# Layer two of a mixture-of-experts kernel: first tile's first two column blocks reordered, last tile computed and stored in halves on three queues

## The chip, the cores and the metric

The kernel runs on one core of one Trainium2 chip. The metric is device microseconds of one execution, median of several; lower is better. The profiled execution is a further one, with the hardware profiler on.

## What is computed

4096 tokens of width 256 pass two layers. Layer one mixes channels, routes each token to two of four experts (capacity 1024 each, exact GELU), and adds the result to x. Layer two, the one that is changed, is a gated feed-forward network whose three matrices each have a low-rank addition that is chosen per sample (32 tokens have one adapter):

```
def _lora_linear(x, W, A, B, adapter_indices):
    base = jnp.einsum('bsd,df->bsf', x, W)
    lora = jnp.einsum('bsr,brf->bsf', jnp.einsum('bsd,bdr->bsr', x, A[adapter_indices]), B[adapter_indices])
    return base + lora
gate = _lora_linear(x, Wg, Ag, Bg, adapter_indices)      # 256 -> 1024, rank 16
up = _lora_linear(x, Wu, Au, Bu, adapter_indices)
h = jax.nn.silu(gate) * up
cond = _lora_linear(h, Wd, Ad, Bd, adapter_indices)      # 1024 -> 256
x = x + (cond @ (weight * scale_weight[:, None]).T + bias)
```

## The kernel before, in words

Every engine has its instruction list written out by hand in its own function; semaphores tie them together. Nothing is scheduled by a tool: the order in the code is the order on the engine.

Layer two takes the tokens in 8 tiles of 512 (BT), sorted by adapter so that a tile has at most two adapters. A tile's 1024 hidden columns are taken in 8 column blocks of 128 (KH). The last linear layer is folded into Wd beforehand. Every float32 product is made of three matmuls, high part by high part, high by low, low by high (`product`, L1207 to L1213), so a block's gate costs 6 matmuls of 512 columns (two halves k of the 256 inputs), its up 6, each plus one low-rank matmul (`pair_half`, L1458), and its part of the down product another 6 (`down1_`).

PSUM has 8 banks of 128x512. Gate blocks alternate between banks 0 and 1, up blocks between 2 and 3, the tile's output (two halves of 128 rows) is gathered in banks 4 and 5, bank 6 takes the low-rank part of down, bank 7 the transposes and the low-rank product `um` of the next tile.

**Start of layer two.** The first tile's input x1T[0] is layer one's last output. PE forms it by 16 matmuls with a 0/1 matrix `pick` (`from_last`, L1517) into banks 0 and 1, DVE adds the token rows (L1190), ACT makes the high part x1s_hi (L717), DVE the low part x1s_lo (L1121). Then PE works through block 0 (banks 0 and 2: L1528, L1529, L1535), the low-rank product (`low_rank`, L1432, L1433, into bank 7), block 1's gate (bank 1) and up (bank 3), with block 0's and 1's `pair_half` in between. The moving operands of `pair_half`, ug and uu, are made from bank 7: DVE masks it (um, L1116), ACT copies 32-row pieces of um into four row groups (three copies for ug, L695 to L697, then three for uu), DVE subtracts to get one further row group of each (L1133). The gate of a block goes through Silu on ACT (L705), DVE multiplies it with the up block (prod, L1168), and splits it in two (L1172, L1174). Block 2 reuses bank 0, so PE waits for the first product before it.

**End of layer two.** After the last tile's blocks PE makes the low-rank down product (`low_rank_down`, L1423), the down product of blocks 6 and 7, and the closing low-rank matmuls (`finish`, L1480 to L1482). DVE adds the bias and x1T (`finish_out`, L1151) into out_sb, one instruction for each half of the rows. Then `last_stores` stores 16 samples (32 tokens each, 256 rows of 32 floats, 32 KB) with one DMA each to a place read from a table: 8 from SP's queue, 8 from ACT's, all behind the same wait on out_ev. POOL is done by then; its DMAs, all indirect gathers and scatters (L458, L469, L488, L496, L504, L518), end some 75 us before the end. SP ends the program when all stores have landed.

The names printed by the profile leave buffer numbers out, and its x_sb, x_rows, x_first in this layer are the code's x1_sb, x1_rows, x1_first.

## Time and profile before

| | us |
|---|---|
| median of 3 runs | 615.31 |
| lowest and highest run | 614.7, 615.56 |
| the profiled execution's own time | 613.93 |
| its span, first to last instruction | 612.1 |
| PE busy in the span | 580.1 (95%) |
| DVE, ACT, POOL busy | 355.0, 241.9, 146.3 |
| mean granted TensorE clock | 0.974 |

The profiled execution is 1.83 us longer than its span, and 1.38 us below the median of the runs. Busy time is summed over instructions; matmuls overlap their neighbours, so that a row's duration of 0.39 us is longer than the distance to the next matmul, and it is the distance that counts. PEld is the load of the stationary operand.

### The profile page before, as it was taken

The numbers are of one execution on the slowest core, as the hardware profiler recorded it, in microseconds if no ns is written. First come the engines' busy times: TensorE is split into PE (matmuls) and PEld (weight loads), VectorE is DVE, ScalarE is ACT, GpSimd is POOL, SyncE is SP. The second block draws the span as 40 slices with busy tenths as digits, with TensorE's granted clock in tenths as the row PEclk, the third lists the DMA queues.
The fourth block names the chain that finished last, engine by engine and source line by source line (L and its number), as shares of the span: only waits on it lengthen the run. The fifth ranks groups of instructions, "written<-read, shape, count | busy, mean of one in ns | idle before, by whom it ended". The sixth has DMA issues, their size and how long they took to land.

```text
span 612.1 us, 9927 instructions
## 1 busy us (share of the span) xinstructions
PE 580.1 (95%) x3438; PEld 476.8 (78%) x3438; DVE 355.0 (58%) x794; ACT 241.9 (40%) x532; POOL 146.3 (24%) x127
## 2 busy tenths in 40 slices
PE   5777699999999999999999999999999999999995
PEld 3645589999999999987878878878788788788783
DVE  6888655875677566655545545544465454544533
ACT  2643146755874764654412412313224133123010
POOL 3000222463454451757004003031040040100000
PEclk9976889999999999999999999999999999999998
DMA  9995749335329321653004105023041050130012
GB/s 326 343 288 180 289 147 325 46 107 136 36 74 315 44 49 22 128 115 95 9 1 138 18 0 146 12 90 66 0 135 19 0 142 13 43 74 6 12 24 34
DMA packets 64988, 61.95 MB, mean 101 GB/s; under 512 B 37616, under 2 KB 56816, under 8 KB 63600
## 3 DMA queue, kind: packets, MB, share of 16 engines
q1 hardware_dynamic: 53168, 37.99, 20.7%
q0 software_dynamic: 9600, 23.14, 15.7%
q10 hardware_dynamic: 2176, 0.26, 0.3%
q8 instruction: 24, 0.39, 0.3%
q14 instruction: 20, 0.16, 0.1%
HBM read 46.10 MB, written 19.47 MB: 107 GB/s over the span
## 4 chain that ended last, share of the span: by engine, by line
PE 87%; DVE 6%; DMA 3%; ACT 1%; issue 1%; SPq 1%; DVEq 0%; POOLq 0%
PE bank L1211 25%; PE bank L1212 24%; PE bank L1213 24%; PE bank L1458 5%; PE bank L1423 2%; DMA xT<-in_xT 2%; DVE passed L862 1%; DMA xg<-flat_rows,slot_row 1%; PE bank L1283 1%; PE bank L1415 1%; PE bank L1319 1%; PE bank L1310 1%; PE bank L1432 1%; PE bank L1433 1%; PE bank L1517 1%
## 5 line engine op out<-in xcount | busy, mean ns | idle before, releaser
L705 ACT ACTIVATE act<-bank 128x512 f32<-128x512 f32 x64 | 38.3, 598 | 189.2 <-PE bank L1458 189.2
L1168 DVE TENSOR_TENSOR prod<-bank,act 128x512 f32<-128x512 f32 x64 | 44.2, 690 | 99.4 <-PE bank L1458 97.3
L1071 DVE TENSOR_TENSOR hid_lo<-hf,hid_hi 128x512 fp32r<-128x512 f32 (+1 forms) x72 | 45.5, 633 | 53.6 <-ACT hf L641 53.3
L1211 PE MATMUL bank<-w_hi,hid_hi 128*128 128x256 f32 x256 | 71.8, 280 | 0.0
L1212 PE MATMUL bank<-w_lo,hid_hi 128*128 128x256 f32 x256 | 71.4, 279 | 0.0
L1213 PE MATMUL bank<-w_hi,hid_lo 128*128 128x256 f32 x256 | 71.3, 279 | 0.0
L638 ACT ACTIVATE hid_hi<-bank 128x512 fp32r<-128x512 f32 (+1 forms) x72 | 39.7, 552 | 67.4 <-PE bank L1213 67.0
L458 POOL DMA_INDIRECT xg<-flat_rows,slot_row x32 | 34.4, 1074 | 128.8 <-DVE slot_row L928 78.7
L469 POOL DMA_INDIRECT x_rows<-y_sb,slot_row x32 | 52.3, 1634 | 43.5 <-ACT y_sb L609 32.7
L1211 PE MATMUL bank<-xs_hi,w_hi 128*128 128x512 f32 (+1 forms) x148 | 56.3, 381 | 1.7 <-DVE xs_lo L938 1.7
L488 POOL DMA_INDIRECT b_pair<-b_rows,b_row x8 | 7.9, 987 | 199.0 <-PE bank L1482 198.4
L1213 PE MATMUL bank<-xs_hi,w_lo 128*128 128x512 f32 (+1 forms) x148 | 54.6, 369 | 0.0
L1212 PE MATMUL bank<-xs_lo,w_hi 128*128 128x512 f32 (+1 forms) x148 | 54.5, 368 | 0.0
L1211 PE MATMUL bank<-x1s_hi,wg_hi 128*128 128x512 f32 x126 | 50.4, 400 | 0.5 <-DVE prod L1168 0.5
L1211 PE MATMUL bank<-hid_hi,wd_hi 128*128 128x512 f32 x128 | 50.8, 397 | 0.0
L1212 PEld LDWEIGHTS bank<-w_lo,hid_hi 128*128 128x128 f32 x256 | 48.2, 188 | 2.3
L1212 PE MATMUL bank<-hid_lo,wd_hi 128*128 128x512 f32 x128 | 50.0, 390 | 0.0
L1213 PE MATMUL bank<-hid_hi,wd_lo 128*128 128x512 f32 x128 | 49.9, 390 | 0.0
L1211 PEld LDWEIGHTS bank<-w_hi,hid_hi 128*128 128x128 f32 x256 | 48.1, 188 | 2.3
L1212 PE MATMUL bank<-x1s_lo,wg_hi 128*128 128x512 f32 x126 | 49.3, 392 | 0.0
L1213 PE MATMUL bank<-x1s_hi,wg_lo 128*128 128x512 f32 x126 | 49.1, 390 | 0.0
L1213 PE MATMUL bank<-x1s_hi,wu_lo 128*128 128x512 f32 x126 | 49.1, 390 | 0.0
(281 smaller groups left out, 1252.1 us busy)
## 6 DMA issues: line engine op xcount, KB each, us to landing
w_raw<-in_L_ffn_W SPq DMA_DIRECT2D x8, 1024.0 KB, 7.3
flat_rows<-x_sb SPq DMA_DIRECT2D x8, 520.0 KB, 10.0
xT<-in_xT SPq DMA_DIRECT2D x8, 512.0 KB, 7.8
x_sb<-in_x SPq DMA_DIRECT2D x8, 512.0 KB, 8.6
outT<-out_sb SPq DMA_DIRECT2D x120, 32.0 KB
wdT<-in_wdT SPq DMA_DIRECT2D x1, 1024.0 KB, 6.2
wg_lo_raw<-in_L_cond_Wg SPq DMA_DIRECT2D x1, 1024.0 KB, 4.8
wu_lo_raw<-in_L_cond_Wu SPq DMA_DIRECT2D x1, 1024.0 KB, 7.1
```

Source lines behind the costliest of these rows:

```text
L458: pool.indirect_dma_start(out=xg[:, q, :], out_offset=None, in_=flat_rows[:, :], in_offset=bass.IndirectOffsetOnAxis(ap=slot_row[:, e, hal ...
L469: pool.indirect_dma_start(out=x1_rows[:, :], out_offset=bass.IndirectOffsetOnAxis(ap=slot_row[:, e, half * GB + q:half * GB + q + 1], axis=0),
L488: pool.indirect_dma_start(out=b_pair[t % 2][:, :].bitcast(f32), out_offset=None, in_=b_rows[:, :], in_offset=bass.IndirectOffsetOnAxis(ap= ...
L638: act.activation(hid[s % 4][0][:, n], bank[s % 2][:, n], ACT.Gelu)
L705: act.activation(act1[h % 2][:, :], bank[h % 2][:, :], ACT.Silu).then_inc(silu1, 1)
L1071: dve.tensor_tensor(lo[:, n], hf[s % 2][:, n], hi[:, n].bitcast(f32), ALU.subtract).then_inc(hid0, 1)
L1168: dve.tensor_tensor(prod[par][h][:, :], bank[2 + h % 2][:, :], act1[h % 2][:, :], ALU.mult).then_inc(prod1, 1)
L1211: pe.matmul(out, lh, rh, start=start, stop=False, skip_group_check=True)
L1212: pe.matmul(out, lh, rl, start=False, stop=False, skip_group_check=True)
L1213: return pe.matmul(out, ll, rh, start=False, stop=stop, skip_group_check=True)
L1423: last = pe.matmul(bank[6][r, :], ad_pair[par][:, h, :], prod[par][h][:, :], start=h < 4, stop=h >= 4, skip_group_check=True, tile_positio ...
L1458: pe.matmul(out[:, :], b_pair[par][:, i * HID + h * P:i * HID + (h + 1) * P], u[:, :], start=False, stop=True, skip_group_check=True).then ...
```

## The change

1. Start. `from_last` now writes banks 4 and 5, and the first block pair is done in another order: high-part products of block 0 and block 1 with the first half of the inputs, then block 0 with the second half, the low-rank product, block 0's low-part products, block 1's rest, and then the four `pair_half` matmuls together (gate 0, gate 1, up 0, up 1). Block 2's gate waits for the first Silu instead of the first product; the wait for that product stands ahead of block 2's up.
2. DVE makes uu's three copies of the first tile (`first_uu`), ahead of its two subtractions; ACT makes ug's only. In all other tiles ACT makes all six, with the waits' counts moved by one.
3. End. In the last tile the down product and the closing matmuls run in two halves of 256 columns: half 0 in banks 4 and 5, half 1 in bank 7 (both row halves). Half 0 is finished, with its DVE additions, before half 1's last block. Its 8 samples are stored from SP (3), ACT (3) and POOL (2), and so are half 1's.

```diff
+        def last_out(j, k):
+            return bank[7][:, k * BT // 2:(k + 1) * BT // 2] if j else bank[4 + k][:, 0:BT // 2]
...
-        def last_stores(queue, side):
-            t = NB1 - 1
-            mine = range(side * SB // 2, (side + 1) * SB // 2)
...
-            queue.wait_ge(out_ev, KD * NB1)
-            for i, s_ in zip(mine, to):
-                queue.dma_start(out_v[:, :, bass.ds(s_, 1), :], out_sb[1][:, :, i * 32:(i + 1) * 32].unsqueeze(2)
-                                ).then_inc(out_done[1], 16)
+        def last_stores(queue, side, done):
+            t, n = NB1 - 1, SB // 2
+            first = (0, 3, 6, n)
+            mine = [[j * n + i for i in range(first[side], first[side + 1])] for j in range(2)]
...
+            for j in range(2):
+                queue.wait_ge(out_ev, KD * (NB1 + j))
+                for i, s_ in zip(mine[j], to[j]):
+                    queue.dma_start(out_v[:, :, bass.ds(s_, 1), :], out_sb[1][:, :, i * 32:(i + 1) * 32].unsqueeze(2)
+                                    ).then_inc(done, 16)
...
-            sp.wait_ge(out_done[1], 16 * SB * NB1 // 2)
+            sp.wait_ge(out_done[1], 16 * SB * (NB1 // 2 - 1) + 16 * 2 * 6)
+            sp.wait_ge(pool_done, 16 * 2 * 2)
...
+            last_stores(pool, 2, pool_done)
...
+            def first_uu():
+                dve.wait_ge(u_ev, 1)
+                dve.tensor_copy(uu[0][32:64, :], um[32:64, :]).then_inc(uu_hi, 1)
+                dve.tensor_copy(uu[0][0:32, :], um[32:64, :])
+                dve.tensor_copy(uu[0][96:128, :], um[96:128, :])
+                dve.wait_ge(u_hi, 1)
+                dve.tensor_tensor(ug[0][64:96, :], um[0:32, :], ug[0][0:32, :].bitcast(f32), ALU.subtract).then_inc(u_lo, 1)
+                dve.wait_ge(uu_hi, 1)
+                dve.tensor_tensor(uu[0][64:96, :], um[32:64, :], uu[0][32:64, :].bitcast(f32), ALU.subtract).then_inc(uu_first, 1)
...
+            def finish_last(wait_store):
...
+                for j in range(2):
+                    c = slice(j * BT // 2, (j + 1) * BT // 2)
+                    for k in range(KD):
+                        dve.wait_ge(acc1, NB1 + (KD if j else k))
+                        dve.scalar_tensor_tensor(out_sb[1][:, k, c], last_out(j, k), out_bias[:, k:k + 1],
+                                                 x1T[1][:, k, c], ALU.add, ALU.add).then_inc(out_ev, 1)
...
-                dve.tensor_tensor(x1T[0][:, k, :], bank[k][:, :], x1T_first[:, k, :], ALU.add).then_inc(x1_sum, 1)
+                dve.tensor_tensor(x1T[0][:, k, :], bank[4 + k][:, :], x1T_first[:, k, :], ALU.add).then_inc(x1_sum, 1)
...
+            def down_last(h, j):
+                s, c = KH * (NB1 - 1) + h, slice(j * BT // 2, (j + 1) * BT // 2)
...
+                for k in range(KD):
...
+                    last = product(last_out(j, k), at(wd, every, h, slice(k * P, (k + 1) * P)), at(hid1[h % 4], every, c),
+                                   start=h == 0 and (j == 0 or k == 0), stop=False)
...
+                    if first and h == 2:
+                        pe.wait_ge(silu1, 1)
...
+            pe.wait_ge(x1_act, 1)
+            for h in range(2):
+                first_hi(0, h)
+            pe.wait_ge(x1_act, KD)
+            first_hi(1, 0)
             pe.wait_ge(x1_lo, KD)
             pe.wait_ge(a_in, 1)
             low_rank(0)
...
+            first_lo(0)
+            first_hi(1, 1)
+            first_lo(1)
+            for h in range(2):
+                pair_half(0, 0, 0, ug[0], bank[h], h, gate1, 0)
+            for h in range(2):
+                pair_half(0, 0, 1, uu[0], bank[2 + h], h, up1, 0)
...
-            down1_(KH * NB1 - 2, KH - 2, NB1 - 1, 1, False, ends=True)
-            down1_(KH * NB1 - 1, KH - 1, NB1 - 1, 1, False, ends=True)
-            finish(NB1 - 1, 1, NB1 // 2 - 1, halves=True)
+            for j in range(2):
+                down_last(KH - 2, j)
+            for j in range(2):
+                down_last(KH - 1, j)
+                finish_last(j)
```

PE's list at the start of layer two, before (x1s0 is the first tile's input, bank 7 the low-rank product, ug0 and uu0 its masked copies):

```order
L1528 MATMUL bank0<-x1s0_hi_209,wg_hi_69 128x512 [waits x1_act]
L1529 MATMUL bank0<-x1s0_hi_209,wg_lo_70 128x512
L1528 MATMUL bank2<-x1s0_hi_209,wu_hi_71 128x512
L1529 MATMUL bank2<-x1s0_hi_209,wu_lo_72 128x512
L1432 MATMUL bank7<-x1s0_hi_209,a_pair0_124 128x512 [waits a_in,x1_lo]
```

The same place now, from the first wait on x1_act to the second:

```order
L1596 MATMUL bank0<-x1s0_hi_209,wg_hi_69 128x512 [waits x1_act,first_ev]
L1597 MATMUL bank0<-x1s0_hi_209,wg_lo_70 128x512
L1596 MATMUL bank2<-x1s0_hi_209,wu_hi_71 128x512
L1597 MATMUL bank2<-x1s0_hi_209,wu_lo_72 128x512
L1596 MATMUL bank1<-x1s0_hi_209,wg_hi_69 128x512
L1597 MATMUL bank1<-x1s0_hi_209,wg_lo_70 128x512
L1596 MATMUL bank3<-x1s0_hi_209,wu_hi_71 128x512
L1597 MATMUL bank3<-x1s0_hi_209,wu_lo_72 128x512
L1596 MATMUL bank0<-x1s0_hi_209,wg_hi_69 128x512 [waits x1_act]
```

Four matmuls of block 1 (banks 1 and 3) now stand ahead of the second wait on x1_act, where four stood ahead of it before. DVE's list after um, now (before, only the two subtractions stood here, each behind a wait on ACT's u_hi):

```order
L1126 TENSOR_TENSOR um_217<-bank7,pack_f2_50 128x512 [waits u_mm]
L1142 CAST uu0_215<-um_217 32x512 [waits u_ev]
L1143 CAST uu0_215<-um_217 32x512
L1144 CAST uu0_215<-um_217 32x512
L1146 TENSOR_TENSOR ug0_213<-um_217,ug0_213 32x512 [waits u_hi]
L1148 TENSOR_TENSOR uu0_215<-um_217,uu0_215 32x512 [waits uu_hi]
```

Three casts now stand between um and ug's subtraction. POOL's list at its end, now (before, it ended with the gather of bd_pair):

```order
L373 TENSOR_LOAD pack_i_51
L373 ISA x2
L378 ISA [waits out_ev]
L378 DMA outT<-out_sb1_242 128x2x32
L378 ISA
L378 DMA outT<-out_sb1_242 128x2x32
L378 ISA [waits out_ev]
L378 DMA outT<-out_sb1_242 128x2x32
L378 ISA
L378 DMA outT<-out_sb1_242 128x2x32
```

POOL has gained four table reads and four stores, two behind each of the two waits on out_ev; SP's and ACT's lists have 3 and 3 where they had 8 behind one wait.

## Rows read from the trace of the kernel before

**Rows 1.** Page: the chain that ended last, by engine.

```profile
PE 87%; DVE 6%; DMA 3%; ACT 1%; issue 1%; SPq 1%; DVEq 0%; POOLq 0%
```

**Rows 2.** Windows: length, busy PE, PEld, DVE, ACT, POOL, granted clock, DMA share, GB/s.

```profile
270.50:280.40 9.90, 8.33 (x34) 5.53 (x33) 4.78 (x8) 7.09 (x11) 6.06 (x6) 1.00 0.39 70
500.00:598.60 98.60, 98.60 (x455) 78.20 (x453) 47.97 (x78) 23.28 (x44) 2.83 (x3) 1.00 0.13 29
```

**Rows 3.** Timeline, PE, start of layer two: start, duration, instruction, idle before and releaser.

```profile
270.54 0.39 PE L1528 MATMUL bank<-x1s_hi,wg_hi 128*128 128x512 f32 x1
271.22 0.39 PE L1529 MATMUL bank<-x1s_hi,wu_lo 128*128 128x512 f32 x1
272.14 0.50 PE L1528 MATMUL bank<-x1s_hi,wg_hi 128*128 128x512 f32 x1 [0.54 <-ACT x1s_hi L717]
273.87 0.39 PE L1433 MATMUL bank<-x1s_lo,a_pair 128*64 128x512 f32 x1
277.05 0.47 PE L1458 MATMUL bank<-ug,b_pair 128*128 128x512 f32 x1 [0.49 <-ACT ug L697]
278.95 0.50 PE L1458 MATMUL bank<-uu,b_pair 128*128 128x512 f32 x1
280.37 0.50 PE L1211 MATMUL bank<-x1s_hi,wg_hi 128*128 128x512 f32 x1 [0.46 <-DVE prod L1168]
```

**Rows 4.** Timeline, DVE and ACT, the same place.

```profile
271.46 0.63 ACT L717 ACTIVATE x1s_hi<-x1T 128x512 fp32r<-128x512 f32 x1 [1.18 <-DVE x1T L1190]
274.30 0.69 DVE L1116 TENSOR_TENSOR um<-bank,pack_f 128x512 f32<-128x512 f32 x1 [1.48 <-PE bank L1433]
276.32 0.62 ACT L697 ACTIVATE ug<-um 32x512 fp32r<-32x512 f32 x1
277.63 0.68 DVE L1133 TENSOR_TENSOR uu<-um,uu 32x512 fp32r<-32x512 f32 x1 [1.27 <-ACT uu L695]
280.35 0.43 DVE L1172 CAST hid_hi<-prod 128x512 fp32r<-128x512 f32 x1
```

**Rows 5.** Timeline, layer one's end: first and 25th of PE's 256-column matmuls; DVE.

```profile
262.28 0.28 PE L1213 MATMUL bank<-xs_hi,w_lo 128*128 128x256 f32 x1
265.07 0.28 PE L1213 MATMUL bank<-w_hi,hid_lo 128*128 128x256 f32 x1
...
267.24 0.88 DVE L1059 SCALAR_TENSOR_TENSOR y_last_lo<-bank,slot_p,y_last_hi 128x256 fp32r<-128x256 f32 x2
```

**Rows 6.** Timeline of the end; last row: ns min/median/max, first and last start.

```profile
601.87 0.69 DVE L1142 TENSOR_TENSOR vs<-vm,vm_hi 128x512 fp32r<-128x512 f32 x1
604.41 1.41 DVE L1151 SCALAR_TENSOR_TENSOR out_sb<-bank,pack_f,x1T 128x512 f32<-128x512 f32 x2 [1.85 <-PE bank L1482]
604.60 0.39 PE L1482 MATMUL bank<-vs,bd_pair 128*128 128x512 f32 x1
605.99 4.26 SPq L370 DMA_DIRECT2D outT<-out_sb  x8
...
L370 ACTq DMA_DIRECT2D outT<-out_sb x8: 397/400/467, 606.0 to 610.0; - x8
```

**Rows 7.** Windows of the end, before, during and after the stores' data.

```profile
606.50:606.75 0.25, 0.00 (x0) 0.00 (x0) 0.00 (x0) 0.00 (x0) 0.00 (x0) 1.00 0.00 0
606.75:611.25 4.50, 0.00 (x0) 0.00 (x0) 0.00 (x0) 0.00 (x0) 0.00 (x0) 0.62 0.76 117
611.25:612.10 0.85, 0.00 (x0) 0.00 (x0) 0.00 (x0) 0.00 (x0) 0.00 (x0) 0.50 0.00 0
```

**Rows 8.** POOL: groups by form, one issue, and the window in which its data starts.

```profile
L469 POOL DMA_INDIRECT x_rows<-y_sb,slot_row x32 | 52.3, 1634 | 43.5 <-ACT y_sb L609 32.7 <-issue 7.0 <-DMA x_first<-x_rows,x_row 3.8
L496 POOL DMA_INDIRECT bd_pair<-bd_rows,bd_row x16 | 15.1, 946 | 4.9 <-issue 4.9
...
531.83 0.94 POOL L488 DMA_INDIRECT b_pair<-b_rows,b_row  x1 [32.94 <-PE bank L1482]
...
533.50:533.75 0.25, 0.25 (x3) 0.21 (x2) 0.25 (x1) 0.00 (x0) 0.25 (x1) 1.00 0.97 164
```

More of the change, by code:

```diff
@@ L306, in adaln_moe_lora @@
         acc1, out_ev = sem("acc1"), sem("out_ev")
-        out_done = [sem(f"out_done{i}") for i in range(2)]
+        out_done, pool_done = [sem(f"out_done{i}") for i in range(2)], sem("pool_done")
         b_out, packed_in, placed, ids_mm, ids_in = (sem("b_out"), sem("packed_in"), sem("placed"), sem("ids_mm"),
@@ L1459, in pair_half, with down1_ @@
                           skip_group_check=True).then_inc(done, 1)
[L1461 to L1466 removed]
+            def down1_(s, h, t, par, first):
+                pe.wait_ge(prod1, s + 2)
                 for k in range(KD):
@@ L1472, in down1_, with finish_last, finish @@
                 last.then_inc(down1, 1)
-            def finish(t, par, pair, halves=False):
+            def down_last(h, j):
+                s, c = KH * (NB1 - 1) + h, slice(j * BT // 2, (j + 1) * BT // 2)
+                if h >= KH - 2:
+                    pe.wait_ge(hid1_s, s + 1)
+                else:
+                    pe.wait_ge(prod1, s + 2)
+                for k in range(KD):
+                    if h == 0 and j == 0:
+                        pe.wait_ge(out_ev, KD * (NB1 - 2) + k + 1)
+                    last = product(last_out(j, k), at(wd, every, h, slice(k * P, (k + 1) * P)), at(hid1[h % 4], every, c),
+                                   start=h == 0 and (j == 0 or k == 0), stop=False)
+                if j:
+                    last.then_inc(down1, 1)
+            def finish_last(j):
+                par, c = 1, slice(j * BT // 2, (j + 1) * BT // 2)
+                pe.wait_ge(v_lo, NB1)
+                pe.wait_ge(bd_in[par], 32 * (NB1 // 2))
+                for k in range(KD):
+                    bd_hi, bd_lo = (bd_pair[par][:, i, k * P:(k + 1) * P] for i in range(2))
+                    pe.matmul(last_out(j, k), bd_hi, vm_hi[:, c], start=False, stop=False, skip_group_check=True)
+                    pe.matmul(last_out(j, k), bd_lo, vm_hi[:, c], start=False, stop=False, skip_group_check=True)
+                    last = pe.matmul(last_out(j, k), bd_hi, vs[:, c], start=False, stop=True, skip_group_check=True)
+                    if not j or k == KD - 1:
+                        last.then_inc(acc1, 1)
+            def finish(t, par, pair):
                 pe.wait_ge(v_lo, t + 1)
@@ L1482, in finish @@
                     last = pe.matmul(bank[4 + k][:, :], bd_hi, vs[:, :], start=False, stop=True, skip_group_check=True)
-                    if halves or k == KD - 1:
-                        last.then_inc(acc1, 1)
+                last.then_inc(acc1, 1)
             def steps1(t, par, pair, first, last):
@@ L1501, in steps1 @@
                         low_rank_down(t - 1, 1 - par, range(KH))
-                    if h >= 2:
+                    if h >= 2 and last:
+                        for j in range(2):
+                            down_last(h - 2, j)
+                    elif h >= 2:
                         down1_(s - 2, h - 2, t, par, first)
                     elif not first:
-                        down1_(s - 2, KH - 2 + h, t - 1, 1 - par, False)
+                        down1_(s - 2, KH - 2 + h, t - 1, 1 - par, first)
                     if not last:
@@ L1523, in _, with first_hi, first_lo @@
                 from_last(k)
-            hc = slice(0, P)
-            for k in range(KD):
-                pe.wait_ge(x1_act, k + 1)
+            def first_hi(k, h):
+                hc = slice(h * P, (h + 1) * P)
                 for i, (w_hi, w_lo) in enumerate((wg, wu)):
-                    pe.matmul(bank[2 * i][:, :], w_hi[:, k, hc], x1s[0][0][:, k, :], start=k == 0, stop=False, skip_group_check=True)
-                    pe.matmul(bank[2 * i][:, :], w_lo[:, k, hc], x1s[0][0][:, k, :], start=False, stop=False, skip_group_check=True)
+                    out = bank[2 * i + h][:, :]
+                    pe.matmul(out, w_hi[:, k, hc], x1s[0][0][:, k, :], start=k == 0, stop=False, skip_group_check=True)
+                    pe.matmul(out, w_lo[:, k, hc], x1s[0][0][:, k, :], start=False, stop=False, skip_group_check=True)
+            def first_lo(h):
+                hc = slice(h * P, (h + 1) * P)
+                for i, (w_hi, _) in enumerate((wg, wu)):
+                    for k in range(KD):
+                        pe.matmul(bank[2 * i + h][:, :], w_hi[:, k, hc], x1s[0][1][:, k, :], start=False, stop=False,
+                                  skip_group_check=True)
+            pe.wait_ge(first_ev, KD)
+            pe.wait_ge(x1_act, 1)
[3 more added lines that the diff above has]
+            first_hi(1, 0)
             pe.wait_ge(x1_lo, KD)
@@ L1532, in _ @@
             low_rank(0)
-            for i, (w_hi, _) in enumerate((wg, wu)):
-                for k in range(KD):
-                    pe.matmul(bank[2 * i][:, :], w_hi[:, k, hc], x1s[0][1][:, k, :], start=False, stop=False, skip_group_check=True)
-            base_half(wg, 0, bank[1], 1)
-            pe.wait_ge(first_ev, KD)
-            pair_half(0, 0, 0, ug[0], bank[0], 0, gate1, 0)
-            base_half(wu, 0, bank[3], 1)
+            first_lo(0)
[5 more added lines that the diff above has]
+                pair_half(0, 0, 1, uu[0], bank[2 + h], h, up1, 0)
             steps1(0, 0, 0, True, False)
```

63 lines of the change are left out of this document (34 added, 29 removed).

## The prediction

> **What bounds the kernel now.** I read the chain of waits first: PE is 87% of it, DVE 6% [rows 1]. So a stage is worth what PE's stream loses in it. The windows tell where that is: from 500 to 598.6 us PE is busy for the whole 98.6, at a granted clock of 1.00, while in the 9.9 us at the start of layer two it is busy for 8.33 [rows 2]. Inside layer two there is nothing to win by waiting less; at its two ends there is.
>
> The timeline of the start shows four stalls. Matmuls of 512 columns begin 0.227 us apart when nothing holds them (270.54 to 271.22 is three steps). The fifth could begin at 271.45 and begins at 272.14, behind ACT's high part of the second input half; later PE waits for ACT's third copy of ug (277.05), for the third of uu (278.95), and for DVE's first product (280.37) [rows 3]. A matmul behind a wait lasts 0.50 and not 0.39, so the next comes 0.11 later.
>
> The end: DVE's two additions end at 604.41 + 1.41 = 605.82, the first store is issued at 605.99, the last at 610.0, eight to a queue and so 0.56 apart [rows 6]. Data flows from about 606.8 to 611.25 with the DMA engines busy 0.76 of the time, 3.4 us for 16 stores, and 0.85 us behind the data the span ends at 612.10 [rows 7]. From the last issue to the end is 2.1 us.
>
> **The start, step by step.** The number of matmuls up to block 2 is unchanged, 32 of 512 columns; their order is new. Eight now stand ahead of the second x1_act wait: 270.54 + 8 x 0.227 = 272.36, and ACT has its part at 271.46 + 0.63 = 272.09 [rows 4], so the first stall is gone. Four more, then the low-rank four, whose last begins at 273.95 where it was 273.87 [rows 3]. So um begins at 274.38, was 274.30 [rows 4]. Twelve matmuls run under it, to 276.90. ACT's ug copies end 0.08 later than now, at 277.02. On DVE three casts now stand ahead of ug's subtraction. The trace of before has none of 32x512. The cast of 128x512 takes 0.43, the subtraction of 32x512 takes 0.68 [rows 4], and a 128x512 operation takes 0.69, so length follows columns and not rows; I take 0.45 a cast with the step to the next, since it is the same operation. They end at 276.45, ug's subtraction at 277.17, which is now later than ACT: PE goes on at 277.27 (it needed 0.11 before). The two gates run; uu's subtraction ends at 277.89, the ups begin at 278.00, and block 2 follows in stride at 278.00 + 0.34 + 0.23 = 278.57. The first Silu ends one gate matmul (0.47 [rows 3]) and one ACT operation (0.63 [rows 4]) behind 277.27, at 278.4, in time for block 2, and the product is asked for only seven matmuls later. Block 2 now begins at 280.37 and loses 0.11 more, together 280.48. **Gain 1.9 us.** Bounds: 1.2 if a cast costs what the subtraction costs (0.68 three times), 2.7 if no wait is left (276.90 + 4 x 0.227). Moving `from_last` to banks 4 and 5 costs nothing: the rows of those banks were read before it. Behind block 2 nothing takes the gain back, as PE is busy without a gap from 280.4 on, and POOL's and SP's later work is released by PE and DVE.
>
> **The end, step by step.** The last tile's 48 down products and 6 closing matmuls of 512 columns become pairs of 256. From 262.28 to 265.07 are 24 such steps, 0.116 each [rows 5]; a pair costs 0.232 against 0.227, so 54 pairs cost 0.3 us. The last matmul then begins at about 605.0 (from 604.60 [rows 6], plus 0.3 and one half step), is 0.11 shorter, and DVE's two additions of 256 columns take 0.88, as two like it do [rows 5], to 606.26: 0.44 later than now. The first half is 12 matmuls earlier and complete at 604.5. Its closing matmuls need vs, done at 601.87 + 0.69 = 602.56 [rows 6], well ahead of 603.0.
>
> Stores of the first half are issued from 604.67 and those of the second from 606.43, with the 0.17 that the issue takes now. On SP and ACT the third of the second half starts at 607.55, and with today's 2.1 behind it the end is 609.65. The DMA engines' work says the same: data from 0.8 behind the issue, half of 3.4 us, and 0.85 to the end give 609.8.
>
> POOL is another matter, and the changed program has nothing like it in the trace of before: a plain store of 256 runs of 128 bytes. Call its time on POOL G. A further DMA follows 0.30 behind the last (4.9 us for 16), data starts 0.73 behind the instruction's end (531.83 + 0.94 = 532.77 to 533.50) [rows 8]; transfer takes about 0.3. POOL issues four in a row, as the second pair's wait is over before it comes to it. The end is 604.67 + 3 x (G + 0.30) + G + 0.73 + 0.3 + 0.85 = 607.45 + 4G. Nearest rows: gathers of 128 rows take 0.95, whatever their bytes, scatters with an addition 1.63 [rows 8]. A store has neither an index list nor an addition, but twice the pieces. I take G = 1.1, near the gather, and keep 0.6 and 1.63 as ends. That gives 611.85: **POOL's last store, not SP's, ends the kernel**, and the whole rebuilding of the end gains a quarter of a microsecond.
>
> The gathers' 0.95 is the same for 1 KB rows and for 8 KB rows [rows 8], and shows nothing for more pieces. The Trainium skill, page "DMA: Bandwidth & Descriptors", section "Anatomy of one DMA — SWDGE (gpsimd) path", states that descriptor generation is small and that many can be emitted before the cost shows. By that rule G stays at 0.95 and the sum would be 0.6 us lower, 612.55; the trace shows neither for 256 pieces.
>
> **Sum.** The span changes by (607.45 + 4G - 612.10) - 1.9, which is 4G - 6.55; with G = 1.1 that is -2.15 us: span 609.95, profiled time 611.8 from 613.93. The median of the runs shown is 615.31, 1.38 above the profiled one; I apply the same difference: **613.2 us**. About 0.2% (1.23 us) is what a measurement of this kernel can tell from no change. The break-even is G = 1.64, faster beyond 0.2% needs G under 1.33.
>
> **Rivals.**
> - *SP and ACT end last.* If POOL is quick (G under 0.6), the end is 609.8 and the change is -2.3 - 1.9 = -4.2: 611.1. For it: SP and ACT issue the same store every 0.56 [rows 6]. Against: no POOL DMA of the trace is under 0.94. The engines bound it here: with 0.76 of their time busy on two queues there is little room for a third. The Trainium skill, same page, section "Issuing engines are not separate DMA queues", says that issuing from more engines saves only the sequencers' time; by that rule this is the floor. Chance 0.10.
> - *The casts are slow.* ug's subtraction waits behind them, and at 0.68 each the start gains 1.2: 613.9. Against: the one cast of the trace takes 0.43. Chance 0.10.
> - *No difference.* POOL takes as long for 256 pieces as for a scatter, G from 1.33 to 1.95, and the stores' delay eats the start's gain: about 615.3 at 1.63. For it: 128 pieces may be half the cost. Chance 0.13.
> - *Slower.* POOL's time grows with its pieces: double 0.95 is 1.9, double the scatter's 1.63 is 3.3. At G = 2.2 the change is +2.25: 617.5. It decides from G = 1.95 on, where four stores in a row push the end past what the start gains by 1.23. Against: rows of very unlike size cost the same, so the fixed part is large. Chance 0.07.
>
> **How the numbers follow.** My forecast, G from 0.9 to 1.33 with the start's full gain, has 0.60. Faster is 0.60 + 0.10 + 0.10 = 0.80, no difference 0.13, slower 0.07. The range reaches from the floor, 611.1, to just under the break-even, 615.2; it leaves out the slower case and the upper part of the one without difference.
>
> **What would show it.** In the changed kernel's timeline block 2's first matmul should begin near 278.6, with no wait for x1s_hi, short ones (0.2 to 0.4) at the first ug and the first uu matmul, and three casts of about 0.43 on DVE. If ug waits for DVE's subtraction the queueing is as I say; if PE still stalls for prod, the order was not what mattered. At the end I expect pairs 0.01 dearer than today's matmuls, a first store issued 1.3 us ahead of today's place (and 3.2 with the start's shift), and four POOL stores of about 1.1 us at a distance of 1.4; the last data should be POOL's (its software queue), some 2 us behind SP's and ACT's. I am wrong if POOL's rows are near 0.5 or over 1.6, if PE waits at the halves (for vs or for banks), or if the shift of 1.9 us seen at block 2 is no longer there at the last tile.

## The result and the profile after

The changed kernel takes 616.85 us (median of 6 runs, 616.11 to 617.32), the kernel before beside it 614.91 us (6 runs). The ratio is 1.0038, with a 95% interval from 1.0024 to 1.0051: slower by 2.3 us by the ratio (the two medians lie 1.9 us apart), where 2.1 us less were forecast, and outside the range. Measured once more (after_again, 10 runs against 21) the ratio is 1.0006, interval 0.9997 to 1.0015. Both say that nothing is gained; why they differ is part of what follows.

The profiled execution of the changed kernel took 616.11 us, with a span of 614.4 (before: 612.1) and a granted clock of 0.98. The start of layer two went as forecast. These rows of PE's and DVE's timeline of the changed kernel answer to [rows 3, 4]:

```profile
271.11 0.40 PE L1596 MATMUL bank<-x1s_hi,wg_hi 128*128 128x512 f32 x1
...
277.91 0.70 PE L1495 MATMUL bank<-ug,b_pair 128*128 128x512 f32 x2 [0.23 <-DVE ug L1146]
278.62 0.70 PE L1495 MATMUL bank<-uu,b_pair 128*128 128x512 f32 x2
279.16 0.40 PE L1241 MATMUL bank<-x1s_hi,wg_hi 128*128 128x512 f32 x1
```

```profile
275.70 0.42 DVE L1142 CAST uu<-um 32x512 fp32r<-32x512 f32 x1
276.14 0.48 DVE L1143 CAST uu<-um 32x512 fp32r<-32x512 f32 x1
276.64 0.42 DVE L1144 CAST uu<-um 32x512 fp32r<-32x512 f32 x1
277.08 0.68 DVE L1146 TENSOR_TENSOR ug<-um,ug 32x512 fp32r<-32x512 f32 x1
```

Block 2 begins 8.05 us behind layer two's first matmul, where it was 9.83. The waits for x1s_hi and for prod are gone, the one at ug is 0.23 and ends with DVE's subtraction.

The end is another matter. From the same profile, the timeline of the additions, then the stores' line (ns min/median/max, first and last start), then the closing instructions of the program. Each engine's list ends with a DRAIN and semaphore instructions that the kernel's code doesn't write out; the profile gives them line 73, the `with` that holds the whole kernel.

```profile
603.33 0.88 DVE L1181 SCALAR_TENSOR_TENSOR out_sb<-bank,pack_f,x1T 128x256 f32<-128x256 f32 x2 [0.85 <-PE bank L1532]
605.04 0.88 DVE L1181 SCALAR_TENSOR_TENSOR out_sb<-bank,pack_f,x1T 128x256 f32<-128x256 f32 x2 [0.83 <-PE bank L1532]
```

```profile
L378 SPq DMA_DIRECT2D outT<-out_sb x6: 372/372/373, 604.4 to 607.2; - x6
L378 POOL DMA_DIRECT2D outT<-out_sb x4: 712/744/767, 605.0 to 607.3; - x4
...
DMA to landing us min/median/max: 2.0/2.1/2.2
```

```profile
L73 POOLq DRAIN  x1: 7063/7063/7063, 607.1 to 607.1; - x1
...
L73 SPq DRAIN  x1: 7/7/7, 609.6 to 609.6; - x1
L73 SPq EVENT_SEMAPHORE  x1: 17/17/17, 614.4 to 614.4; - x1
```

POOL's stores are cheap (0.74 us each, landed 2.1 us after their issue), and SP has seen every store land at 609.6. Then for 4.8 us nothing runs: all engines stand at their last semaphore until POOL's closing DRAIN is over at 607.1 + 7.06 = 614.2. POOL's last store ends at 607.3 + 0.7 = 608.0, so that the DRAIN is over 6.2 us behind POOL's last work. The windows of the changed kernel's end show the same, as an answer to [rows 7]: the data is over by 608.75, and what follows is empty.

```profile
608.50:608.75 0.25, 0.00 (x0) 0.00 (x0) 0.00 (x0) 0.00 (x0) 0.00 (x0) 0.50 0.57 139
608.75:609.00 0.25, 0.00 (x0) 0.00 (x0) 0.00 (x0) 0.00 (x0) 0.00 (x0) 0.50 0.06 8
609.00:614.40 5.40, 0.00 (x0) 0.00 (x0) 0.00 (x0) 0.00 (x0) 0.00 (x0) 0.50 0.00 0
```

In the kernel before, the same instruction is there and costs nothing, because POOL's last gather ends at 535.3 (closing instructions of the kernel before):

```profile
L73 POOLq DRAIN  x1: 9772/9772/9772, 531.6 to 531.6; - x1
```

That DRAIN is over at 541.4, again 6.1 us behind POOL's last work and 70 us ahead of the end.

**How the profiles are compared below.** Layer one, which the change leaves alone, differs by up to 1.6 us between profiles of one and the same kernel (layer two's first matmul at 271.61, 270.64 and 270.00 in three profiles of f1_front_only's program). So I use three distances inside a profile, all in us: *start*, from layer two's first matmul to block 2 (before: 280.37 - 270.54 = 9.83); *front*, from the same matmul to the first low-rank down product of tile 0 (46.72); and *tail*, from the last tile's low-rank down product, which precedes the end's new order, to the end of the span (612.1 - 598.69 = 13.4).

```profile
598.69 1.92 PE L1423 MATMUL bank<-prod,ad_pair 128*32 128x512 f32 x16
```

In the changed kernel it begins at 598.61, and the tail is 15.8: 2.4 us longer where the forecast had it 0.25 shorter.

### The profile page after: what moved, and what is told of

Its sections match the earlier page's. It is cut to its first block, busy times and chain, and to the rows that moved or that the text cites. A ratio compares the mean times of both kernels' runs of the same rounds, so it can differ in the third digit from the quotient of the medians.

```text
span 614.4 us, 10041 instructions
## 1 busy us (share of the span) xinstructions
PE 577.6 (94%) x3492; PEld 477.9 (78%) x3492; DVE 356.6 (58%) x799; ACT 239.2 (39%) x529; POOL 150.0 (24%) x131
## 3 DMA queue, kind: packets, MB, share of 16 engines
q10 hardware_dynamic: 1632, 0.20, 0.2%
## 4 chain that ended last, share of the span: by engine, by line
PE 85%; DVE 7%; DMA 3%; issue 1%; another core or an unknown queue 1%; ACT 1%; SPq 1%; POOL 0%; POOLq 0%; DVEq 0%
PE bank L1241 24%; PE bank L1242 23%; PE bank L1243 23%; PE bank L1495 5%; PE bank L1453 2%; DMA xT<-in_xT 2%; DVE passed L872 2%; DMA xg<-flat_rows,slot_row 1%; PE bank L1313 1%; PE bank L1349 1%; PE bank L1445 1%; PE bank L1340 1%; PE bank L1462 1%; PE bank L1463 1%
## 5 line engine op out<-in xcount | busy, mean ns | idle before, releaser
L1241 PE MATMUL bank<-hid_hi,wd_hi 128*128 128x512 f32 (+1 forms) x144 | 53.5, 372 | 0.0
L1242 PE MATMUL bank<-hid_lo,wd_hi 128*128 128x512 f32 (+1 forms) x144 | 52.8, 366 | 0.0
L1243 PE MATMUL bank<-hid_hi,wd_lo 128*128 128x512 f32 (+1 forms) x144 | 52.7, 366 | 0.0
```

Source lines behind the costliest of these rows:

```text
L1241: pe.matmul(out, lh, rh, start=start, stop=False, skip_group_check=True)
L1242: pe.matmul(out, lh, rl, start=False, stop=False, skip_group_check=True)
L1243: return pe.matmul(out, ll, rh, start=False, stop=stop, skip_group_check=True)
```

## The experiments

### The end: what does a store on POOL cost?

Theory: POOL's closing DRAIN takes about 6 us from when POOL has nothing left. Rivals: it waits for POOL's own DMAs; only a late DMA, not any work on POOL, brings it on; the halves themselves cost.

**e1_no_pool**, the changed kernel with POOL's four stores on SP and ACT:

```
-            first = (0, 3, 6, n)
+            first = (0, 4, n)
...
-            last_stores(pool, 2, pool_done)
```

> The changed kernel, with POOL's four stores given to SP and ACT (four each in either half). Theory drain: the program ends when POOL's closing DRAIN is over, which in the changed kernel's profile lasts 7.06 us and ends 6.2 us behind POOL's last store, while SP is done at 609.6. Without a POOL store the DRAIN is hidden again. SP and ACT issue eight stores each from 604.4 at 0.56, the last at 608.3, and the end is 2.1 behind it: 610.4 against 614.4, so 4.0 less than the change and about 2.1 less than before (some 612.8 where before gives 614.9). Theory traffic (the DMA engines are slower with three queues, not POOL as such): at most 1 us below the change, 616.

Measured: 613.46 us (11 runs), ratio 0.9970, interval 0.9958 to 0.9981. The tail is 611.3 - 599.42 = 11.9: 3.9 shorter than the changed kernel's and 1.5 shorter than before's. Closing instructions of this kernel:

```profile
L73 POOLq DRAIN  x1: 9772/9772/9772, 531.8 to 531.8; - x1
...
L73 SPq DRAIN  x1: 7/7/7, 611.1 to 611.1; - x1
```

So the whole loss of the end is in the four stores on POOL. Halves stored on two queues gain at the end, and this kernel beats both others.

**e2_pool_waits**, the changed kernel, where POOL first waits for its stores to land:

```
             last_stores(pool, 2, pool_done)
+            pool.wait_ge(pool_done, 16 * 2 * 2)
```

> The changed kernel, where POOL waits for its own four stores to have landed ahead of its DRAIN. Theory fixed: the DRAIN's end lies 6.2 us behind the last software DMA whatever is waited for: time unchanged, DRAIN shorter (about 5). Theory landing: DRAIN waits for stores that are still under way; with nothing under way it is short and the kernel ends near 610.5, 4 us less. Theory restart: DRAIN takes its 6 to 7 us from when it begins, at about 609.3: end at 615.5 to 616.4, 1 to 2 us more than the change.

Measured: 619.1 us (4 runs), ratio 1.0054, interval 1.0038 to 1.0069; tail 17.4. POOL's stores begin at 607.00, and its closing instruction starts when all has landed, at the moment when SP is through:

```profile
L73 POOLq DRAIN  x1: 6193/6193/6193, 611.6 to 611.6; - x1
...
L73 SPq DRAIN  x1: 7/7/7, 611.7 to 611.7; - x1
```

It still takes 6.19 us. It doesn't wait for the DMAs: it has a length of its own. The 6 us count from the moment at which POOL has nothing left to do or to wait for; here the DRAIN is over 7.8 us behind the last store.

**e4_pool_first_half**, POOL with the first half's two stores only:

```
-            first = (0, 3, 6, n)
+            first = ((0, 3, 6, n), (0, 4, n, n))
...
```

> The changed kernel, POOL stores its two samples of the first half only, the second half is on SP and ACT (four each). Theory drain: POOL's second store ends at about 606.4, its DRAIN at 612.6, while SP ends at 609.9: 1.8 less than the change, near the time of before (615.0). Theory traffic: no more than 0.5 less than the change. If the DRAIN's length goes with the number of POOL stores (two for four), it would end at 610 or before and the kernel be 4 us below the change.

Measured: 615.42 us (10 runs), ratio 1.0001, interval 0.9988 to 1.0015; tail 614.5 - 600.30 = 14.2. POOL is through 1.6 us earlier in the program, and so is the end: 606.67 + 1.51 = 608.2, the DRAIN over at 614.2, 6.0 behind.

```profile
L73 POOLq DRAIN  x1: 6962/6962/6962, 607.3 to 607.3; - x1
...
L73 SPq DRAIN  x1: 7/7/7, 611.4 to 611.4; - x1
```

**e3_before_pool_store**, the kernel before with two of its last 16 stores on POOL, 7 on SP, 7 on ACT:

```
-            mine = range(side * SB // 2, (side + 1) * SB // 2)
+            mine = (range(0, 7), range(7, 14), range(14, 16))[side]
...
+            last_stores(pool, 2)
```

> The kernel before with nothing changed but that two of the last sixteen stores are issued by POOL (7 on SP, 7 on ACT). Theory drain: POOL begins them at 606.5, ends at 608.1, DRAIN 6.2: 614.3 and 614.5 for the end, 2.3 above before. Rival, the slowdown needs the halves or the new start: at most 0.5 from before, either way.

Measured: 616.42 us (5 runs), ratio 1.0038, interval 1.0024 to 1.0052; tail 15.7, and the DRAIN over at 608.1 + 6.96 = 615.1. Two stores in the old program bring the same loss: neither the halves nor the new start is needed for it.

**e5_pool_memset**, the kernel before with one small memset on POOL behind the last addition:

```
+            pool.wait_ge(out_ev, KD * NB1)
+            pool.memset(vm[:, 0:1], 0.0)
```

> The kernel before, POOL waits for the last out_ev and then clears one column of a dead tile: no DMA, but its DRAIN begins at about 606.2 instead of 531.6. With stores of its own, POOL's DRAIN took 6.2 us from the moment it had nothing left to do, even when all of them had landed. Theory any: in this program the closing DRAIN costs 6.2 us whenever it begins (software DMAs were used at some time): DRAIN ends at 612.4, and the kernel is 0.3 to 0.6 us slower than before. Theory recent: only DMAs issued shortly before count: the DRAIN is a few tenths and the time that of before.

Measured: 614.09 us (10 runs) against 613.88, ratio 1.0002, interval 0.9991 to 1.0012. The time doesn't move, but the profile decides: a memset starts the 6 us anew, a late DMA isn't needed. (Every kernel here uses POOL's DMAs earlier on; whether the DRAIN is as long in one without any isn't shown.) Here the DRAIN, over at 611.5, just fits under SP's end, and the 0.3 to 0.6 us that I had expected don't come.

```profile
605.54 0.10 POOL L532 MEMSET vm<- 128x1 f32 x1 [70.60 <-DVE out_sb L1153]
...
L73 POOLq DRAIN  x1: 5983/5983/5983, 605.5 to 605.5; - x1
...
L73 SPq DRAIN  x1: 7/7/7, 611.6 to 611.6; - x1
```

**e6_pool_dma_early**, the kernel before with one spare DMA of 128 KB to scratch rows on POOL, 12 us ahead of the end:

```
+            pool.wait_ge(hid1_s, KH * NB1)
+            pool.dma_start(x1_rows[TOK:TOK + P, :], prod[1][0][:, 0:D]).then_inc(pool_done, 16)
...
```

> The kernel before with one further POOL DMA (128 KB into spare rows that nobody reads) at about 599.4, when the last hidden block is split. Theory: DRAIN ends 6.2 behind it, 606.6, which is before SP's end at 611.9: no difference from before. Rival: a late software DMA delays the end wherever it stands (SP waits for it, queues are shared): 0.5 us or more.

Measured: 614.43 us (10 runs) against 613.88, ratio 1.0004, interval 0.9991 to 1.0017. The DMA is issued at 599.02 in 0.59 us, the DRAIN is over at 599.0 + 6.57 = 605.6, 6.0 behind it and 6 ahead of the end: free.

### The start: how much of the 1.9 us at block 2 reaches the end?

**f1_front_only**, the change's start with the end of before:

```
-            last_stores(sp, 0, out_done[1])
+            last_stores(sp, 0)
...
-            finish_last(16 * SB * (NB1 // 2 - 1))
+            finish_out(NB1 - 1, 1, 16 * SB * (NB1 // 2 - 1), halves=True)
...
```

> The change's start (order of the first two column blocks, DVE's three casts), with the end of the kernel before. The gap from layer two's first matmul to block 2's is 8.05 us in the change and 9.83 plus 0.11 before. Theory: that 1.9 reaches the end in full, 613.0 where before gives 614.9. Rival: it is taken up behind block 2 (by a later wait), and the time is that of before.

Measured: 614.24 us (11 runs), ratio 0.9988, interval 0.9979 to 0.9998. The start is 8.03, 1.8 shorter, but the front only 45.74, 1.0 shorter. Where it goes is in the timeline of this kernel, tile 0, block 3:

```profile
288.81 0.60 ACT L710 ACTIVATE act<-bank 128x512 f32<-128x512 f32 x1 [5.27 <-remote]
...
292.38 0.69 DVE L1194 TENSOR_TENSOR prod<-bank,act 128x512 f32<-128x512 f32 x1 [7.25 <-remote]
```

```profile
293.12 0.50 PE L1237 MATMUL bank<-hid_hi,wd_hi 128*128 128x512 f32 x1 [0.66 <-DVE prod L1194]
```

PE's row of the gate begins at 285.58, yet the Silu that waits for it starts at 288.81. The product follows 3 us after the Silu's end, though the up matmul of 287.16 is long done, and PE then loses 0.8 us. I call this a *late start*. "remote" is the trace's word for a releaser that it doesn't know.

**f2_order_only**, the same with all six copies on ACT:

```
-            u_copies(0, 0, first=True)
+            u_copies(0, 0)
...
-            first_uu()
+            u_low(0, 0)
...
```

> The change's new order at the start, with the end of before and all six copies on ACT as before (no casts on DVE). Block 2's distance from layer two's first matmul: first ug near where it was, uu two copies later (ACT ends its sixth at about 279.0 in the time of before), so block 2 at 279.6 against 280.48: 9.05 us, a gain of 0.9 of the change's 1.9. In the time of the runs no more than 0.9 below before.

Measured: 613.03 us (12 runs) against 613.88, ratio 0.9986, interval 0.9978 to 0.9995; start 9.13, front 46.00, 0.7 shorter. No late start. The order alone is worth 0.7 us in the front and 0.9 in the time, and the waiting for uu that is left shows in PE's timeline:

```profile
279.55 0.70 PE L1492 MATMUL bank<-uu,b_pair 128*128 128x512 f32 x2 [1.25 <-ACT uu L702]
```

Every profile so far with DVE's casts had late starts (f1, the changed kernel, e1, e2, e4), none without. But f1, e1, e2 and e4 were measured together on one chip (number 0), and e3, e5, e6 and f2, all without casts, on another (number 4), so that program and chip weren't told apart. I suspected the programs' length: a place at which an engine's instructions are fetched.

**g1_act_rows**, f1 with three one-column copies on ACT; **g2_dve_rows**, f2 with three one-column memsets on DVE; **g3_dve_shift**, f1 with sixteen memsets at DVE's start:

```
g1: +            for i in range(3):
    +                act.activation(spare[:, i:i + 1], cols[:, 0:1], ACT.Copy)
g2: +            for i in range(3):
    +                dve.memset(spare[:, i:i + 1], 0.0)
g3: +            for i in range(16):
    +                dve.memset(spare[:, i:i + 1], 0.0)
```

> The changed start with the end of before (as f1_front_only), plus three one-column copies on ACT in its idle time behind the Silu warm-up, so that ACT's program is again as many instructions long ahead of tile 0 as in before. In the kernels with DVE's casts, ACT and DVE stand idle between 284.5 and 293 us of their profiles although their operands are complete (f1_front_only: Silu of block 3 at 288.81 where its gate was complete by 286.0, product at 292.38, next copy of x1 at 293.19 where its transposes were complete by 289.3), and TensorE then loses about 0.75 us behind the product. Theory 'program place': an engine runs dry where a block of its instructions is fetched, and where that falls depends on the count of instructions ahead. If ACT's three missing instructions are what shifts it, ACT's two late starts go here and DVE's product may or may not stay late; the gain over before grows from 0.7 to up to 1.4 us (613.6). Theory 'timing': the tile's early steps simply run into POOL's gathers because TensorE is earlier; then this kernel shows the same idle times as f1_front_only and about 614.2 us.

> The new order of the start with all six copies on ACT (as f2_order_only, whose ACT and DVE are never late in tile 0), plus three one-column memsets on DVE ahead of ug's subtraction, so that DVE's program is as long ahead of tile 0 as in f1_front_only. 'Program place' on DVE: DVE's product of block 3 comes 2 to 3 us after its operands are complete (near 290 to 292 us instead of 288.2), TensorE loses about 0.7 us and the kernel is level with before (about 614.9 against 614.9). 'Timing', or program place on ACT alone: no late product, and the same 0.14% gain as f2_order_only (613.9 where before is 614.8).

> f1_front_only with sixteen one-column memsets at DVE's very start, where it waits 3.9 us for its first input, so that the same place of DVE's program is reached sixteen instructions earlier (in the additions behind layer one). 'Program place': DVE's late product of block 3 is gone (it starts within 0.5 us of the Silu's end), and a pause of 2 us or more appears sixteen instructions earlier, in the last hundredths of layer one or at the start of layer two, where it may cost more (up to 2 us) or nothing. 'Timing': the product of block 3 stays 3 us late and nothing else moves, about 0.1% faster than before.

Measured: g1 615.95 us, ratio 1.0007 (0.9994 to 1.0020); g2 616.54, ratio 1.0025 (1.0011 to 1.0039); g3 615.66, ratio 0.9994 (0.9980 to 1.0007), each of 10 runs against the same 25. All three have late starts, with the fronts 45.61, 47.05 and 46.77, g2 too, which has no casts: the casts aren't needed for them. On the face of it g2 supported the suspicion; these three ran on a third chip (15), though, and the kernel before wasn't profiled there. In g3, where the place is moved by sixteen instructions, the late product stays at block 3: moving the place doesn't move it.

**h1_before_rows**, the kernel before with three memsets at DVE's start:

```
+            for i in range(3):
+                dve.memset(spare[:, i:i + 1], 0.0)
```

> The kernel before with three one-column memsets at DVE's very start (where it waits 3.9 us for input) and nothing else: DVE's program is 902 instructions long, as in f1_front_only, instead of 899. Theory 'late starts belong to the program as laid out': ACT's step near 260 us (the copy of hid_hi behind the step in which the first pair columns are made) comes 1 to 1.3 us late as in all kernels with 902 or more, and DVE's product of block 3 near 290 us comes 2 to 3 us late, with a wait of TensorE of about 0.7 us; the time is 0.2 to 0.4% above before. Rival 'they belong to the changed start': no late starts, the same time as before within 0.1%.

Measured: 615.36 us (12 runs) against 614.28, ratio 1.0017, interval 1.0007 to 1.0026. The profile has no late start and a front of 46.72, as before. By itself that doesn't clear the length: f1_again, below, ran on the same chip (13) and had none either. The program is 1.1 us slower all the same. Its profile is 1.0 us longer than before's: 0.8 of that lies ahead of layer two (271.33 against 270.54), which moves by as much between profiles of one program, and 0.2 in the tail (13.6). Why isn't shown.

**f2_again** and **f1_again**, the two programs unchanged, one execution each:

> f2_order_only once more, for its profile. If the late starts come and go from execution to execution, this profile may show them; if they belong to the program, ACT and DVE are on time again near 260 and in tile 0 (product of block 3 8.1 us behind block 2's first matmul), span about 611.8.

> f1_front_only once more, for its profile. If the late starts belong to the program: Silu of block 3 again 9.1 us behind block 2's first matmul (6.4 if on time), the product 12.7 us behind it (8.0 if on time), and TensorE's wait of 0.7 us near 293. If they are chance, this profile may show none and a span of 611.4.

Measured: f2_again 614.50 us, front 46.02, no late start. f1_again 612.33 us against 614.28, **no late start**, front 45.01. The same program had them once and now has none: the program alone doesn't bring them.

**f1_third, f2_third, after_again**, side by side, again unchanged:

> f1_front_only a third time, now timed again. Its first timing gave ratio 0.9988 with late starts of ACT and DVE in the profile, its second profile showed none and a time 1.95 us under the kernel before beside it. If the late starts come and go from one measurement to the next, the ratio moves between measurements (0.9969 without them, 0.9988 with); if they are a property of the program, it is 0.9988 again.

> f2_order_only a third time, timed again beside f1: without late starts it is 1.1 us slower than f1 (ratio 0.9987 against 0.9969). If it is level with f1 again, the late starts were there in most of f1's executions.

> The changed kernel once more: the closing instruction on POOL again ends the span 6.2 us behind POOL's last store and 14.5 us behind the last low-rank down product. If the late starts are absent here, the time is up to 1.2 us under the first measurement (ratio 1.002 instead of 1.0038); it is not faster than before.

Measured against 614.85 (21 runs): f1_third 612.01 us (5 runs), ratio 0.9965, interval 0.9952 to 0.9979; f2_third 613.97 (11), ratio 0.9986 (0.9977 to 0.9995); after_again 615.20 (10), ratio 1.0006, 0.0014 under the lowest that I had expected. None of the three profiles has a late start.

Late starts go with the set of runs. The experiments were measured in five sets, each on another chip, and in the profiles of a set it is all or none:

| chip | profiles | with late starts |
|---|---|---|
| 0 | e1, e2, e4, f1_front_only | all 4 |
| 4 | e3, e5, e6, f2_order_only | none |
| 15 | g1, g2, g3 | all 3 |
| 13 | h1, f2_again, f1_again, b1 | none |
| 8 | f1_third, f2_third, after_again | none |

Chips 13 and 8 had none in programs that had them before, and chip 15 had them in g2, which is f2 with three memsets. Whether it is the chip or the time isn't told apart, as no chip was used twice. For the first profiles of the kernel before (none) and of the changed kernel (late starts) no chip is on record, and the kernel before was never profiled on chip 0 or 15, so that what late starts cost in the ratio isn't shown.

Late starts aren't confined to tile 0. In the same 8 profiles ACT also begins its first copy of the next x1T 2.5 us late in each of the next five tiles, at no cost (the distance from the first tile's to the last one's low-rank down product is the same), and is late in layer one too. These are ACT's rows there, of the changed kernel's first profile and of after_again:

```profile
262.94 0.39 ACT L648 ACTIVATE hid_hi<-bank 128x256 fp32r<-128x256 f32 x1 [2.08 <-PE bank L1243]
...
262.08 0.38 ACT L648 ACTIVATE hid_hi<-bank 128x256 fp32r<-128x256 f32 x1 [0.73 <-PE bank L1243]
```

From y_last_hi (L628, at 257.48 and 257.98) to layer two's first matmul it takes 13.6 us with late starts and 13.1 without; in f1 13.7 against 13.3. So the same program loses 1.0 to 1.1 us by them in what can be located, in layer one and in the front: 0.5 and 0.5 in the changed kernel, 0.4 and 0.7 in f1.

Block 3 in the timeline of f1_third, to be read against f1_front_only's above:

```profile
284.58 0.60 ACT L710 ACTIVATE act<-bank 128x512 f32<-128x512 f32 x1 [2.47 <-PE bank L1491]
286.17 0.69 DVE L1194 TENSOR_TENSOR prod<-bank,act 128x512 f32<-128x512 f32 x1 [2.46 <-PE bank L1491]
```

| | start | Silu of block 3 behind block 2 | product | front |
|---|---|---|---|---|
| before | 9.83 | 6.46 | 8.05 | 46.72 |
| f1_front_only, first | 8.03 | 9.17 | 12.74 | 45.74 |
| f1, third | 8.24 | 6.34 | 7.93 | 45.03 |
| changed kernel, first | 8.05 | 7.71 | 11.26 | 45.50 |
| changed kernel, again | 8.24 | 6.33 | 7.91 | 44.96 |

Without late starts the front is 1.7 us shorter, and the front alone gains 0.35% (2.2 us); with them 1.0 shorter and 0.12%. f2, measured only on chips 4, 13 and 8, gave 0.9986 both times that it was timed. after_again ends as before: its span is 613.9, its tail 613.9 - 598.08 = 15.8, with

```profile
L73 POOLq DRAIN  x1: 7072/7072/7072, 606.6 to 606.6; - x1
```

over at 613.7, and SP through at 609.1.

**b1_order_halves**, e1_no_pool with f2's copies on ACT:

```
-            first_uu()
+            u_low(0, 0)
...
```

> The candidate made of the parts that gained: the new order at the start with all six copies on ACT (as f2_order_only), the last tile in halves, and its stores on SP and ACT only (as e1_no_pool). The start is worth 0.8 us and the end 1.6 less 0.3 for the pairs of 256 columns: 2.1 us, ratio 0.9965. DVE's program is 901 instructions long; if the late starts come with its length, 0.7 to 1.2 us of that is lost here and the ratio is 0.998.

Measured: 612.76 us (12 runs) against 614.28, ratio 0.9974, interval 0.9964 to 0.9984; start 9.13, front 46.02, tail 610.7 - 598.77 = 11.9, no late start. The gains of start and end add up: front -0.7, pairs of 256 columns +0.6, tail -1.5 make 1.6 us, which is what the ratio gives, where 2.1 were expected. e1_no_pool, with DVE's casts and on chip 0, is level with it even though its own profile had late starts (Silu 9.14, product 12.68 behind block 2, front 45.87).

## Why the prediction was wrong

**The step that failed** is the end's: "transfer takes about 0.3 ... The end is 604.67 + 3 x (G + 0.30) + G + 0.73 + 0.3 + 0.85 = 607.45 + 4G". The 0.85 behind the last data was read off a kernel whose end is SP's, and carried over to one in which POOL is last. The closing DRAIN is over 5.9 to 6.2 us behind POOL's last work, in six profiles with stores, a DMA or a memset at the end, and 6.2 behind the end of POOL's wait in e2, and behind the gathers of the kernel before, where it is hidden by 70 us. With it the sum reads: first store at 604.67, four of them 3.01, then 6.2 and the 0.2 from a last DRAIN to the end of the span that both kernels show: 614.1, or 2.0 us more than 612.1. With the start's 1.9 off that is no difference. As 0.2 of the pairs' forecast 0.3 falls ahead of the tail, this sum puts the tail at 1.8 more than before's. It measured 2.4 more; the other 0.6 is that POOL's first store starts 0.77 behind the additions' end (604.98 against 603.33 + 0.88 = 604.21), where the forecast gave it SP's 0.17.

**"POOL's last store ends the kernel": right engine, wrong instruction.** G was 0.74 and not 1.1, and the next store follows at once and not 0.30 later (four in 3.01), so that the stores are seen landed by 609.6. With G = 0.74 the recorded sum gives 610.4 for the end; it measured 614.4, so that the error in G hid part of the missing DRAIN and didn't cause the miss. The rival "slower" was to decide "from G = 1.95 on"; the kernel got slower at G = 0.74, since its mechanism was another.

**SP's and ACT's end: right.** Forecast 609.65 to 609.8, measured 609.6 with the last low-rank product 0.08 earlier than before's. **The additions**: forecast to end at 606.26, measured 605.04 + 0.88 = 605.92. **Pairs of 256**: undersized. Twelve of them in the last tile take 593.88 - 592.45 = 1.43 us, six of 512 in f1_third 1.36, so a pair costs 0.012 more and not 0.005, or 0.6 us for 54. From the first tile's low-rank product to the last one's the halves cost 0.57 us (after 282.00, before 281.43) for 36 pairs, a little over that.

**The start: right to 0.2 us.** Casts 0.42 to 0.48 against my 0.45; block 2 1.8 sooner, plus the 0.11 of its slower first matmul, 1.9; ug waits for DVE and not for ACT. The rival "the casts are slow" is out.

**"Behind block 2 nothing takes the gain back, as PE is busy without a gap"** failed in some sets of runs and held in others. Late starts on ACT and DVE took back 0.5 to 1.8 us of the front in 8 profiles, among them the first of the changed kernel (0.5 us: 45.50 against 44.96), and were absent in 12, among them three repeats of the very same programs. With them, in the changed kernel's first profile, the parts are front -1.2, pairs +0.6, tail +2.4, together +1.7 to +1.8, inside what the first measurement allows (1.5 to 3.1). Without them, in after_again, front is -1.8 and the parts make +1.2, where the second allows -0.2 to +0.9. So 0.3 us or more of the second isn't in the parts, and layer one, whose length varies from profile to profile, is not excluded.

**Open.** What makes a late start. Nothing in the program alone does: neither DVE's casts (g2 has none), nor the earlier start of TensorE (f1_again, f1_third and after_again have it). Instructions that are fetched late aren't shown either: in tile 0 the two packets of the instruction queues come at 285.9 and 295.6 in the changed kernel's first profile and at 285.5 and 292.6 in after_again, the second only behind the late Silu and product; in g3 one came at 282.7 instead, and the late starts stayed where they were. The trace doesn't name the releaser. Nor is it known why three idle memsets cost h1 1.1 us.

## What to carry to other kernels

- Ahead of giving POOL a last piece of work, look where its closing DRAIN ends: about 6.2 us behind POOL's last instruction or wait. As long as POOL is through 6.2 us before the others it costs nothing; later than that every microsecond counts in full (e4 gave POOL its last store 1.6 us earlier in the tail and ended 1.6 us earlier). A memset starts it as well as a store.
- Look up the closing instructions of each engine in the profile, also those that are hidden now, before the order in which engines finish is changed.
- Where 0.3% matter, time the kernel in more than one set of runs and on more than one chip, profile the kernel before in each, and compare distances inside a profile: the same program measured 0.9988 and 0.9965 of the kernel before. A property that follows the chip looks like one of the program as long as each program is seen on one chip.

## What the runs showed of the hardware

- POOL's closing DRAIN is over 5.9 to 6.2 us behind POOL's last work or wait: 6.19 with every DMA landed, 5.9 behind a memset, 6.0 behind one DMA or two stores, 6.2 behind four. In the kernel before SP's took 7 ns, ACT's 0.15 us, DVE's 0.8 and PE's 2.4.
- A plain store of 256 runs of 128 bytes takes 0.71 to 0.77 us on POOL, the next one follows at once (four in 3.01 us), and it lands 2.1 us after its issue; the gathers of 128 rows took 0.95 [rows 8]. So the store cost no more for its 256 runs. But the trace lists 128 packets on POOL's queue for its four stores, 32 a store, and 1632 on SP's for six, 272 a store; that POOL handles 256 pieces at no cost isn't shown. The Trainium skill, page "DMA: Bandwidth & Descriptors", section "Anatomy of one DMA — SWDGE (gpsimd) path", says that generating descriptors is a small part. POOL's instruction takes 0.74 of the 2.1 us here, and no row shows how much of that goes to descriptors.
- A third issuing queue did shorten SP's and ACT's part: from the last low-rank product to SP's end 609.6 - 598.61 = 11.0 us with six stores each, 611.1 - 599.42 = 11.7 with eight (e1). That is less than the two issues of 0.56 [rows 6] that each was spared. The same page, section "Issuing engines are not separate DMA queues", says that only the sequencers' time is saved, and 0.7 us is within it.
- ACT and DVE can start an operation 1 to 6 us after its operands' rows are over: in all seven profiles taken on two chips and in none of the eleven on three others, with one program (f1) on both sides. Block 3's Silu and product and the next copy of x1T are late each time, by amounts that differ (the Silu begins 7.7 to 12.3 us behind block 2, 6.3 to 6.5 without).
